# Two ternary weight matrices made in split steps, and every engine's work in a new order, in a transformer block kernel on one core

## What is computed

```python
def attn_part(x):                       # x: [8, 512, 256], normalised
    n = layer_norm(x, ln1_w, ln1_b)
    Q, K = elu(n @ q_w.T + q_b) + 1, elu(n @ k_w.T + k_b) + 1       # 64 wide
    V = n @ v_w.T + v_b
    a = causal_linear_attention(Q, K, V) @ o_w.T + o_b
    x = x + a
    h = gelu(layer_norm(x, ln2_w, ln2_b) @ f1_w.T + f1_b)           # 1024 wide: "first MLP"
    return x + h @ f2_w.T + f2_b

def ffn_part(x):
    h = gelu(x @ ternary(W_fc).T)                                   # 1024 wide
    return layer_norm(h, ln_w, ln_b) @ ternary(W_proj).T

def ternary(W):                         # -1, 0 or 1 by the mean of |W|
    g = mean(abs(W)) + 1e-6
    return sign(W / g) * minimum(round(abs(W / g)), 1)

x = x + attn_part(norm(x))
x = x + ffn_part(norm(x))
```

## Time and profile before

| | us |
|---|---|
| median of 3 runs | 459.44 |
| lowest and highest of them | 459.27, 460.21 |
| the profiled execution, its own time | 459.38 |
| its span in the trace | 457.6 |
| PE busy in the span | 441.3 |
| DVE busy | 372.4 |
| ACT busy | 323.0 |
| POOL busy | 187.1 |

### The profile page before, as it was taken

The page is one execution under the profiler, slowest core; times in us unless marked ns, Lnnn a source line. Parts: engine busy times, 40 slices in busy tenths (PEclk is TensorE's granted clock), DMA queues, the critical chain, the costliest instruction groups (busy, mean ns, idle before and its releaser), DMA issues.

```text
span 457.6 us, 8944 instructions
## 1 busy us (share of the span) xinstructions
PE 441.3 (96%) x2990; PEld 399.6 (87%) x2990; DVE 372.4 (81%) x1212; ACT 323.0 (71%) x604; POOL 187.1 (41%) x188
## 2 busy tenths in 40 slices
PE   3898999999999999999999999999999999999997
PEld 3786897999989899889989999889998899888977
DVE  6899888867898679986798778987799778876776
ACT  4896856997379854998469963898469885686163
POOL 3887042543247043540537041560536323370333
PEclk9999999999999999999999999999999999999999
DMA  8333000000010002000020002000020000000001
GB/s 237 120 106 127 0 2 1 1 25 1 24 46 25 2 0 70 2 23 1 2 69 2 24 1 69 2 25 1 0 71 2 23 1 9 17 1 23 1 24 47
DMA packets 10061, 14.09 MB, mean 31 GB/s; under 512 B 800, under 2 KB 9120, under 8 KB 9504
## 3 DMA queue, kind: packets, MB, share of 16 engines
q1 hardware_dynamic: 10016, 13.52, 8.9%
...
## 4 chain that ended last, share of the span: by engine, by line
PE 83%; issue 5%; DVE 4%; POOL 2%; DMA 2%; ACT 1%; SPq 1%; POOLq 0%; ACTq 0%
PE bank_f L425 13%; PE bank_p L473 11%; PE bank_y L208 6%; PE bank_y L209 6%; PE bank_y L439 6%; PE bank_y L210 6%; PE bank_f L208 5%; PE bank_f L209 5%; PE bank_f L210 5%; PE bank_a L208 4%; PE bank_a L210 4%; PE bank_a L209 4%; PE bank_a L216 2%; DMA x_odd<-in_x 2%; PE bank_f L216 2%
## 5 line engine op out<-in xcount | busy, mean ns | idle before, releaser
L1188 POOL TENSOR_TENSOR rs<-ve,neg_half 128x2 f32<-128x2 f32 x48 | 33.7, 702 | 204.0 <-DVE ve L872 196.6
L208 PE MATMUL bank_y<-wf_hi,h_hi 128*128 128x256 f32 x240 | 67.2, 280 | 0.0
L209 PE MATMUL bank_y<-wf_lo,h_hi 128*128 128x256 f32 x240 | 67.1, 280 | 0.0
L210 PE MATMUL bank_y<-wf_hi,h_lo 128*128 128x256 f32 x240 | 67.1, 279 | 0.0
L933 DVE TENSOR_TENSOR h_lo<-bank_f,h_hi 128x512 fp32r<-128x512 f32 x60 | 41.2, 686 | 27.5 <-ACT h_hi L686 27.4
L473 PE MATMUL bank_p<-wpj_t,g_hi 128*128 128x256 f32 x240 | 60.6, 288 | 0.0
L678 ACT ACTIVATE bank_f<-bank_f,f_bias 128x512 f32<-128x512 f32 x64 | 42.3, 661 | 25.4 <-PE bank_f L210 24.9
L1068 DVE SCALAR_TENSOR_TENSOR g_lo<-bank_y,vec,g_hi 128x256 fp32r<-128x256 f32 x128 | 55.0, 476 | 4.5 <-ACT g_hi L715 4.1
L473 PE MATMUL bank_p<-wpj_t,g_lo 128*128 128x256 f32 x240 | 58.6, 280 | 0.0
L715 ACT ACTIVATE g_hi<-bank_y,vec 128x256 fp32r<-128x256 f32 x128 | 53.5, 477 | 7.2 <-PE bank_y L439 3.8
L425 PE MATMUL bank_f<-wfc_t,z3T_hi 128*128 128x512 f32 x128 | 53.7, 420 | 0.8 <-DVE z3T_lo L933 0.8
...
## 6 DMA issues: line engine op xcount, KB each, us to landing
...
```

What stands on the lines that cost most here:

```text
L208: pe.matmul(ps, w[0], r[0], start=start, stop=False, skip_group_check=skip)
L209: pe.matmul(ps, w[0], r[1], start=False, stop=False, skip_group_check=skip)
L210: return pe.matmul(ps, w[1], r[0], start=False, stop=stop, skip_group_check=skip)
L1188: pool.tensor_tensor(rs[n][:, 2 * h:2 * h + 2], ve[n][:, 2 * h:2 * h + 2], neg_half[:, 0:2], ALU.pow).then_inc(s[f"ln{n + 1}_rs"], 1)
```

## The change

`ternary(n)` is cut in two calls. `tern_low(n)` waits for the threshold and for the slab before, and makes the comparison into the scratch; `ternary(n)` then only waits for that and makes the weights. The instructions themselves are the same, and other calls may now stand between the two:

```diff
-            def ternary(n):
-                w, k = n // 2, n % 2
-                raw = (fc_raw, pj_raw)[w][:, k, :]
-                dst = wfc[:, k, :] if w == 0 else wpj[:, 4 * k:4 * k + 4, :].rearrange("p m d -> p (m d)")
+            def ternary_raw(n):
+                return (fc_raw, pj_raw)[n // 2][:, n % 2, :]
+
+            def tern_low(n):
+                w = n // 2
                 dve.wait_ge(s["theta_ready"], 3 * w + 3)
                 if n == 0:
                     dve.wait_ge(s["wf2_lo"], 4)
-                if n:
+                else:
                     dve.wait_ge(s["tern"], n)
-                dve.tensor_scalar(scratch, raw, theta[:, 2 + w:3 + w], None, ALU.is_lt).then_inc(s["low"], 1)
+                dve.tensor_scalar(scratch, ternary_raw(n), theta[:, 2 + w:3 + w], None, ALU.is_lt).then_inc(s["low"], 1)
+
+            def ternary(n):
+                w, k = n // 2, n % 2
+                dst = wfc[:, k, :] if w == 0 else wpj[:, 4 * k:4 * k + 4, :].rearrange("p m d -> p (m d)")
                 dve.wait_ge(s["low"], n + 1)
-                dve.scalar_tensor_tensor(dst, raw, theta[:, w:w + 1], scratch, ALU.is_gt, ALU.subtract).then_inc(s["tern"], 1)
+                dve.scalar_tensor_tensor(dst, ternary_raw(n), theta[:, w:w + 1], scratch,
+                                         ALU.is_gt, ALU.subtract).then_inc(s["tern"], 1)
```

Besides, the call lists of PE, ACT, DVE and POOL are written anew, in `first()`, `step(g)` and `last()`. No call is added or dropped but the four halves. Of PE's list these lines bear on the prediction:

```diff
             def first():
...
-                attend(0, 0); attend(0, 1); attend(0, 2); tu(1, 0); attend(0, 3); tu(1, 1); f1b(); tz2(0, 0)
-                tz2(0, 1); qk_mm(1); f1(0, 0); theta_sum(0); f1(0, 1); f1(0, 2); f2(0, 0); f1(0, 3); theta_sum(1)
+                attend(0, 0); attend(0, 1); attend(0, 2); attend(0, 3); tu(1, 0); f1b(); tu(1, 1); theta_sum(0)
+                tz2(0, 0); tz2(0, 1); f1(0, 0); f1(0, 1); qk_mm(1); f1(0, 2); theta_sum(1); f1(0, 3); f2(0, 0)
...
             def step(g):
...
-                tr(g, 0, 0); tr(g, 0, 1); fc(g, 2, 0); tz2(g + 1, 0); fc(g, 2, 1); fc(g, 3, 0); tr(g, 0, 2)
-                proj(g, 0, 0); tr(g, 0, 3); tz2(g + 1, 1); fc(g, 3, 1); proj(g, 0, 1); tr(g, 1, 0)
+                fc(g, 2, 0); tr(g, 0, 0); tr(g, 0, 1); fc(g, 2, 1); tz2(g + 1, 0); fc(g, 3, 0); proj(g, 0, 0)
+                tr(g, 0, 2); proj(g, 0, 1); tz2(g + 1, 1); tr(g, 0, 3); fc(g, 3, 1); tr(g, 1, 0)
```

More of the change, by code:

```diff
@@ L505, in last @@
[L505 to L514, removed]
+                proj(5, 0, 2); f1(6, 0); tu(7, 0); f1(6, 1); proj(5, 0, 3); tr(5, 1, 1); tr(5, 1, 2); tu(7, 1)
@@ new lines, in last @@
+                f1(6, 2); f1(6, 3); proj(5, 1, 0); qk_mm(7); tr(5, 1, 3); f1(6, 4); f1(6, 5); f2(6, 0); f2(6, 1)
+                f2(6, 2); f1(6, 6); f2(6, 3); f1(6, 7); scores(7); f2(6, 4); f2(6, 5); f2(6, 6); f2(6, 7)
+                v_mm(7, 0); v_mm(7, 1); proj(5, 1, 1); proj(5, 1, 2); proj(5, 1, 3); attend(7, 0); attend(7, 1)
+                attend(7, 2); tz3(6, 0); tz3(6, 1); attend(7, 3); fc(6, 0, 0); fc(6, 0, 1); fc(6, 1, 0); fc(6, 1, 1)
+                tr(6, 0, 0); fc(6, 2, 0); tr(6, 0, 1); fc(6, 2, 1); tz2(7, 0); fc(6, 3, 0); tr(6, 0, 2)
@@ L718, in first @@
             def first():
[L720 to L729, removed]
@@ L1092, in first @@
-                ln2_var(0, 0); u_lo(1, 0); attn_out(0, 2); attn_out(0, 3); ln2_stats(0, 2); ln2_stats(0, 3)
-                ln2_var(0, 1); ln2_shift(0, 0); z2_odd(0, 0); ln2_shift(0, 1); z2_odd(0, 1); u_lo(1, 1)
-                f1_bias_add(); z2_lo(0, 0); z2_lo(0, 1); qk_max(1); ln3_lo(); n1_shift(1); threshold(0); h_lo(0, 0)
-                ternary(0); h_lo(0, 1); ternary(1); h_lo(0, 2); threshold(1); h_lo(0, 3); ternary(2); ternary(3)
-                qk_sum(1); h_lo(0, 4); selectors(); qk_lo(1); h_lo(0, 5); ln1_stats(2, 0); af_mask(1)
@@ new lines, in first @@
+                consts(); ln1_stats(0, 0); ln1_stats(0, 1); dcol(); ln1_shift(0, 0); u_odd(0, 0); ln1_shift(0, 1)
+                qk_bias_add(); u_odd(0, 1); n1_ve(0); wide_cols(); u_lo(0, 0); u_lo(0, 1); wqk_lo(); n1_shift(0)
+                ln1_stats(1, 0); qk_max(0); qk_sum(0); wvo_add(); ln1_shift(1, 0); qk_lo(0); wvo_lo()
+                ln1_stats(1, 1); af_mask(0); ae_mask(0); ad_mask(0); af_lo(0); n1_ve(1); ae_lo(0); v_lo(0, 0)
+                ad_lo(0); v_lo(0, 1); attn_out(0, 0); ln1_shift(1, 1); attn_out(0, 1); ln2_stats(0, 0)
@@ new lines, in first @@
+                attn_out(0, 2); ln2_stats(0, 1); attn_out(0, 3); ln2_stats(0, 2); ln2_var(0, 0); ln2_stats(0, 3)
+                ln2_var(0, 1); ln2_shift(0, 0); u_lo(1, 0); z2_odd(0, 0); ln2_shift(0, 1); ln3_lo(); z2_odd(0, 1)
+                threshold(0); n1_shift(1); z2_lo(0, 0); z2_lo(0, 1); u_lo(1, 1); tern_low(0); f1_bias_add()
+                ternary(0); h_lo(0, 0); tern_low(1); h_lo(0, 1); ternary(1); threshold(1); h_lo(0, 2); tern_low(2)
+                qk_max(1); ternary(2); h_lo(0, 3); tern_low(3); ternary(3); qk_sum(1); h_lo(0, 4); selectors()
```

177 lines of the change are left out of this document (94 added, 83 removed).

## The result

| | before | after |
|---|---|---|
| time, us: median (lowest to highest, runs) | 459.27 (458.92 to 460.21, 6) | 461.53 (461.01 to 461.72, 6) |
| profiled execution: time, span | 459.38, 457.6 | 461.70, 460.0 |
| granted clock, mean of the span | 1.000 | 0.996 |

The ratio after to before is 1.0036, 95% interval 1.0022 to 1.0051: the changed kernel is 0.36% **slower**, some 1.7 us. The forecast was +0.15% with the chance of slower at 0.35. The median stands 0.4 over the range's upper end; the ratio times the 459.44 from which the sum started is 461.1, just on that end.

What follows compares the result with a forecast made beforehand. PE was taken to set the loop's time, leaving only its 16.3 us of idle time to gain. Head and first MLP +0.5, ternary product -0.2, loop +0.45, last part 0, on 459.38, gave 460.1 us, range 458.9 to 461.1.

Steps and rivals of the forecast that it cites:

- chance of slower: Whole kernel: chance 0.35 that the time lies over 460.4 us, the upper end of what counts as the same.
- Scores at 19.1: Sequence 0's attention: with the statistics moved away, the first scores start at 19.1 instead of 19.55, 0.42 us earlier.
- covered: DVE in the head: the moved statistics, 1.25 us, end some 20.9 behind `wvo_lo`, hidden by the scores.
- The second `z2_odd`: Ahead of `f1(0, 0)`: DVE and POOL take turns into SBUF, so it is done at 34.5 and `f1(0, 0)` starts at 36.7.
- slower rival (2): DVE's `ln3_lo` and second `z2_odd`, 32 to 35.5 us: POOL takes every turn, one further `wf2_lo`; 460.8 us, chance 0.13.
- The first MLP: From `f1(0, 0)`: `qk_mm(1)`, 1.40 us, is still to do, `theta_sum(0)`, 0.14, is done; the split ternary gives 1.54 back.
- 1.54 given back: Ahead of `f1(0, 2)` and `f1(0, 3)`: split ternary returns 2.24 + 0.1 - 0.8 us of idle time.
- The idle time that I had put at 0.66: Ahead of `f1(0, 2)`: it starts at 41.7, where PE was free at 41.04.
- The 0.14 ahead of `f1(0, 3)`: First MLP: `f1(0, 3)` loses another 0.14 us, in the same way as `f1(0, 2)`.
- The first ternary product: `fc(0, 0, 0)` ahead of `tz3(0, 1)`: fills part of the wait for `z3T_lo`; -0.2 us, bounds -0.5 and +0.3.
- the loop: New `step(g)`: `fc(g, 2, 0)` directly follows `fc(g, 1, 1)`, costing 0.09 us in each of five steps; +0.45, bounds 0 and 1.5.
- the end: Last part: two groups of transposes fewer, -0.18, but first `fc(7, 0, 0)` later; 0 in all, bounds -0.3 and +0.4.

Runs made afterwards that it cites:

- e10: The changed kernel run once more, unaltered, for its distribution over the granted clock: 461.64 us, ratio to the kernel before 1.0037.
- e13: Kernel before with ternary weights split, `ln3_lo` late, `h_lo(0, 2)` between the second slab's calls, whole chain of second statistics moved: 460.63 us, ratio to before 1.0010.
- e3: Changed kernel plus eleven matmuls whose result nobody reads, keeping PE busy around `tz2(0, 1)`: 460.66 us, ratio to the kernel before 1.0023.
- e2: Kernel before's first part with the changed kernel's `step(g)` and `last()`: 459.88 us, ratio to the kernel before 1.0007.

## Why the prediction was right or wrong

**The head.** "Scores at 19.1": 19.55 in the profiled execution, 19.04 in e10's. DVE in order of time, of before and then of after:

```profile
12.95 0.75 DVE L885 BATCH_NORM_STATS2 bn<-x_odd 128x6 f32<-128x256 f32 x2 [1.33 <-DMA x_odd<-in_x]
14.21 0.74 DVE L946 TENSOR_SCALAR qk_relu<-bank_p,qk_bias 128x512 f32<-128x512 f32 x1
```
```profile
13.38 0.75 DVE L892 BATCH_NORM_STATS2 bn<-x_odd 128x6 f32<-128x256 f32 x2 [1.33 <-DMA x_odd<-in_x]
14.64 0.74 DVE L953 TENSOR_SCALAR qk_relu<-bank_p,qk_bias 128x512 f32<-128x512 f32 x1
```

From `qk_relu` to the scores it is 5.34 before and 4.91 after, -0.43 as reckoned; the input of this execution landed 0.43 later and hid it. Over the fourteen profiles the scores lie between 18.65 and 20.00, so a step of 0.4 can't be read from one. That the statistics would be "covered" by the scores was wrong in kind: the masks pay. In the changed kernel, which moves the rest of the chain and the order of the masks too, that is only 0.09 (`attend(0, 0)` 4.49 after the scores, 4.40 before); in e13 it is 0.68.

**The second `z2_odd`: the step that failed.** I put it at 34.5, as two of four ways in which the turns might fall out. It ended at 35.77, of which 0.4 is the late input and 1.0 the further turn, and from `z2_odd` to `f1(0, 0)` it then took the 2.2 that I had. The mechanism, the place and the price per turn (1.0) were right; the number of turns was wrong. This was my slower rival (2), down to its condition: POOL starts first (31.82 against 31.83) and again between the parts. I had given it 0.13, too little by my own rows: in the earlier trace rows it was DVE that was slowed at each `wf2_lo`, and POOL only in the slab, at `xpb` and `xs`. The Trainium skill, "SBUF — State Buffer", section "Who interferes with whom", says that whoever issues first has the port; the trace agrees on who waits, but the hold shown is again 1.0 (1.41 less 0.41) of 1.27, not the whole instruction. The term's size: from the scores to `f1(0, 0)` I had 36.7 less 19.1, 17.6 us; it was 18.40, so **0.8 more**.

**The first MLP.** Forecast from `f1(0, 0)` to `attend(1, 0)`: 1.26 for `qk_mm(1)` less `theta_sum`, 1.54 given back: -0.28. In e3, where the clock held, that stretch is 31.93 against 32.39: **-0.46**, 0.2 better, in pieces of some 0.1 that I can't name. The idle time that I had put at 0.66 shows there, too: `f1(0, 2)` starts 0.70 late. The 0.14 ahead of `f1(0, 3)` doesn't: between the two stands only `theta_sum(1)`. The first slab's halves ran at 1.61 and 2.18 (in the changed kernel) as said. What the sum lacked is the clock: +0.62 in the profiled execution (32.55 less 31.93), +1.5 in e10's. The forecast has no term for it, and that is a second step that failed: it moves `qk_mm(1)` out of the gap and leaves the clock at 1.00, without a reason. My own numbers had PE nearly idle from `tu(1, 1)` to 36.7; I looked only at what each wait costs by itself.

**The first ternary product, the loop and the end.** These lie behind `attend(1, 0)`. Forecast: -0.2, +0.45 and 0, together +0.25. Measured: +0.22. The agreement is partly luck: e2, which has the loop and the end alone, shows +0.27 where the forecast has +0.45, so the product gave 0.05 in this pair where 0.2 was forecast. A step is 52.90 us, not 52.95: a loss is there, but it is 0.04 a step, half of the 0.09.

**Sum.** 460.1 + 0.8 (turns) + 0.6 (clock) - 0.2 (first MLP) + 0.4 (late input) = 461.7, the profiled execution's own time. The late input is no part of the change: without it the pair of profiles differs by 2.0 us, where the ratio says 1.7. The sign was a matter of two causes in the same 6 us, and one of them I had as a rival with too small a chance; the range reached it only just.
